# A two-layer graph network kernel: the residual sum ahead of the gated products on VectorE, and TensorE's output banks released by the gated products

## The chip, the cores and the metric

One core of one Trainium2 chip runs the whole kernel. The metric is the device time of one execution in microseconds, as the median over runs. The engines are TensorE (PE in the profile, PEld for its weight loads), VectorE (DVE), ScalarE (ACT), GpSimd (POOL) and SyncE (SP). Each runs its own stream of instructions in order, and they are tied together by semaphores: one engine's instruction raises one when it completes, another engine's stream waits for a count.

## The reference, cut to what matters

There are 50,000 nodes with 160 features (64 scalars and 32 vectors of 3) and 50,000 edges sorted by destination. Two layers follow each other, each with a layer norm and a ReLU in front.

```python
h = maximum(layernorm(x), 0)
x = x + L0(h, edge_attr_4, edge_attr_8)     # first layer, gated
h = maximum(layernorm(x), 0)
x = x + L1(h, node_vec1, edge_attr_4, edge_attr_10)

# L0, cut:
xs, xv = s @ W1_s, v @ W1_v                 # of the node rows
w = silu(edge_embed @ fc_w1 + b1) @ fc_w2 + b2
msg = [products of w, xs[src], xv[src] and edge_sh]     # 384 per edge
agg = segment_sum(msg, dst)
out_s, out_v = agg_s @ W2_s + s @ Wsc_s, agg_v @ W2_v + v @ Wsc_v
scalars, gates = silu(out_s[:, :64]), silu(out_s[:, 64:96])
return node_features + [scalars, out_v * gates]
```

The change is in the end of the first layer: `out_v * gates` is the gated product, and `x + node_features` is the residual sum that the new rows start from.

## The kernel before, in words

The code counts its layers from 0 (`first` is true in the layer that the change is about). The node range is cut into 10 lanes, and one turn handles a pair of tiles, 128 edges each, of two lanes. There are 205 turns, and after them a short second pass (`finish`, `t.serial`) for destinations with too many edges.

The turns are a software pipeline written out by hand. `run_steps` calls `step(T)` once for each step s on each engine, and `T(k)` is turn s-k, or nothing where that doesn't exist. So in one step an engine works on several turns at different stages, and the order of the lines in `step` is the order of its stream.

In the first layer a turn goes through these stages. T(0): the gathered rows `xg` and the node rows `xn` are in, VectorE takes their statistics (`stats`, `means`) and subtracts the mean (`edge_h`, L1138), GpSimd makes the inverse deviations (`rstd`). T(1): ScalarE makes the node's normed rows `hn` (`node_h`, L1404) and TensorE transposes (`transposes`). T(2): TensorE computes the radial hidden layer (`radial`, L1567) and the edge products (`edges`), ScalarE copies them to SBUF (`copy_xw`: L1422, then two scaled pieces in L1429), VectorE adds `xn` and `hn` into `kept` (`residual`, L1148). T(3): VectorE makes the messages (`products` from L1214 on, `messages`). T(4): TensorE sums them by destination (`sums`). T(5): TensorE multiplies the sums by the output weights (`outputs`, L1622) into `out_ps`, and ScalarE takes the SiLU of the gates and scalars (`gates`, L1458). T(6): VectorE multiplies the vectors by the gates (`gated_vectors`, L1241, which reads `out_ps`, the last reader of its first 192 columns), and adds the result to the residual sum (`new_rows`, L1251, which reads SBUF alone); then statistics for the second layer's norm (`stats2`, `means2`, with GpSimd's `rstd2`, L1082 and L1084). T(7): VectorE's `scales2` (L1281), ScalarE's `node_h2`, TensorE's `transposes2` (L1639). T(8): TensorE's `pre` (L1651) makes the second layer's node products in other columns of the same banks, ScalarE scales them out (`scale_pre`, L1483) and stores them (`base_tab`, issued on its own queue, L1511). T(9): SP stores the new rows to `table` (L968).

`kept` has 8 slots (`RING`). `residual` overwrites a slot, so it waits for the stores of the turn 8 before (`stored[t.slot]`), and for `hn_ready`. `outputs` has to wait until `out_ps` is free: in the first layer `deep` is 1, so it waits for the `rows_ready` of the turn before, which `new_rows` raises. `pre` waits for `rows_ready` of a turn that `outputs`, just ahead of it in the same step, has waited for already. `gated_ready` is raised by `gated_vectors`; before, only `new_rows` waits for it.

Every third step up to step 123, VectorE also advances the plan of the lanes in pieces between the other work: `lanes.reach` (needs a gather of GpSimd), `clip`, `count`, `advance`, `keep`. Each piece waits for the piece before it.

## Time and profile before

| | us |
|---|---|
| median of 3 runs | 2412.83 |
| lowest and highest | 2403.69, 2425.43 |
| the profiled execution | 2389.98 |
| its span, first to last instruction | 2388.2 |

Over the span TensorE is busy for 91%, its weight loads for 86%, ScalarE 81%, VectorE 80%, GpSimd 65%. The first layer's turns run from about 60 us to 1500 us, the second layer's from about 1560 us to the end. The granted TensorE clock is 0.968 of full speed over the span (2.4 GHz is full), and 0.99 to 1.00 from 400 us to 1500 us.

How to read the rows that follow: a timeline row has the start in us from the span's first instruction, the busy time in us, the engine, the line of the kernel, the operation, its tiles as out<-in, and the count merged into the row. A bracket at its end is time in which the engine stood idle just before, with what ended it. Where a row merges two or more instructions of an engine, the time is of all of them together. Starts on one engine can be closer than the busy times, since the next instruction starts while the last one completes.

### The profile page before, as it was taken

To read this page: it belongs to the slowest core of one execution; us is meant where nothing else is said; L and a number is where in the kernel's file an instruction comes from. 1 tells how busy PE (TensorE), PEld (TensorE's weight loads), DVE (VectorE), ACT (ScalarE), POOL (GpSimd) and SP (SyncE) were. 2 spreads that over 40 slices of the span, in tenths; PEclk is the share of its full clock that TensorE was granted. 3 is DMA by queue.
4 is the path that set the end of the run, shared out by engine and by line. 5 is a ranking of instruction groups with operands and counts; after the bars stand their busy time and mean duration, and the time that the engine had idled before them with its cause. 6 is when DMAs were issued, how large, how long until landed. Compare 5 with 4: busy or idle time off the path is not lost. (4 is left out here: it accounts for less than half of the span.)

```text
span 2388.2 us, 79221 instructions
## 1 busy us (share of the span) xinstructions
PE 2176.7 (91%) x22003; PEld 2045.3 (86%) x22004; DVE 1909.6 (80%) x8636; ACT 1930.8 (81%) x5167; POOL 1541.1 (65%) x1925
## 2 busy tenths in 40 slices
PE   0889999999999999999999999559999999999997
PEld 0788888889999899899999999359999998999996
DVE  5878998789899898898889988227777777777775
ACT  2677898788888888798889988338888888888885
POOL 4766888778878887777777776145555554554550
PEclk9999999999999999999999999669999999999998
DMA  5456557644445545444444443247777776776772
GB/s 156 90 147 146 142 146 204 175 125 131 126 129 132 125 131 134 116 132 132 132 127 132 133 131 105 64 111 191 190 189 191 190 188 178 189 186 176 197 189 76
DMA packets 498819, 351.30 MB, mean 147 GB/s; under 512 B 188108, under 2 KB 484030, under 8 KB 498382
## 3 DMA queue, kind: packets, MB, share of 16 engines
q1 hardware_dynamic: 401007, 209.61, 34.3%
q0 software_dynamic: 41472, 69.42, 13.0%
q10 hardware_dynamic: 55904, 67.22, 8.1%
q8 instruction: 182, 2.98, 0.5%
q14 instruction: 254, 2.08, 0.3%
HBM read 199.00 MB, written 151.77 MB: 147 GB/s over the span
## 5 line engine op out<-in xcount | busy, mean ns | idle before, releaser
L1060 POOL DMA_INDIRECT xg<-table,from_row x411 | 397.9, 968 | 422.3 <-DVE msg L1233 229.1
L1622 PE MATMUL out_ps<-w_out,aggT 128*128 128x128 f32 (+1 forms) x4932 | 604.6, 273 | 17.4 <-issue 14.3
L1622 PEld LDWEIGHTS out_ps<-w_out,aggT 128*128 128x128 f32 x4932 | 591.6, 194 | 21.3 <-issue 19.4
L1060 POOL DMA_INDIRECT xg<-in_x,win x411 | 484.7, 1179 | 148.8 <-issue 127.5
L1607 PE MATMUL agg_ps<-sel,msg 128*128 128x128 f32 x3708 | 525.9, 284 | 27.5 <-issue 16.0
L1607 PEld LDWEIGHTS agg_ps<-sel,msg 128*128 128x128 f32 x3708 | 463.4, 195 | 37.0 <-issue 25.2
L1438 ACT ACTIVATE msg<-pw,win 128x64 f32<-128x64 f32 x1233 | 341.3, 352 | 5.2 <-issue 2.9
L1449 ACT COPY aggT<-agg_ps 128x768 f32<-128x768 f32 (+1 forms) x310 | 247.4, 798 | 96.0 <-PE agg_ps L1607 56.6
L1073 POOL TENSOR_TENSOR rs<-ve,neghalf 128x4 f32<-128x4 f32 x206 | 224.2, 1088 | 17.1
L1404 ACT ACTIVATE hn<-xn,nmr,rs 128x192 f32<-128x192 f32 x411 | 201.2, 540 | 41.5 <-DVE nmr L1165 41.2
L1483 ACT ACTIVATE kept<-out_ps,a_sb 128x320 f32<-128x320 f32 x410 | 193.9, 525 | 49.0 <-PE out_ps L1651 35.0
L1422 ACT COPY xw_sb<-front_ps 128x512 f32<-128x512 f32 x206 | 120.6, 586 | 112.4 <-PE front_ps L1639 91.1
L1082 POOL TENSOR_SCALAR ve<-mv 128x2 f32<-128x2 f32 x206 | 76.8, 373 | 205.3 <-DVE mv L1274 170.4
L1466 ACT ACTIVATE h<-kept,nmr,rs 128x192 f32<-128x192 f32 x411 | 201.7, 546 | 3.6 <-DVE nmr L1281 3.6
L1257 DVE SCALAR_TENSOR_TENSOR kept<-out_ps,a_sb,kept 128x160 f32<-128x160 f32 x410 | 138.4, 379 | 73.3 <-PE out_ps L1622 37.5
L1241 DVE TENSOR_TENSOR fe<-out_ps,fe 128x192 f32<-128x192 f32 x206 | 73.4, 356 | 150.4 <-ACT fe L1458 143.1
L1592 PE MATMUL front_ps<-w_fc,hid 100*128 100x192 f32 x822 | 182.2, 345 | 11.0 <-issue 10.0
L1651 PE MATMUL out_ps<-w_pre,hT 64*128 64x128 f32 (+1 forms) x2466 | 185.3, 281 | 5.8 <-ACT hT L1475 5.3
L1583 PE MATMUL front_ps<-w_lin,hT 64*128 64x64 f32 (+1 forms) x2466 | 174.9, 273 | 8.0 <-issue 3.8
L1629 PE MATMUL out_ps<-w_sc,hT 64*128 64x96 f32 (+2 forms) x2466 | 179.8, 278 | 0.0
L1084 POOL TENSOR_TENSOR rs<-ve,neghalf 128x2 f32<-128x2 f32 x206 | 168.1, 816 | 17.2
L1607 PE MATMUL front_ps<-sel,msg 128*128 128x128 f32 x1224 | 161.5, 282 | 17.1 <-issue 13.2
(194 smaller groups left out, 5039.2 us busy)
## 6 DMA issues: line engine op xcount, KB each, us to landing
base_tab<-kept ACTq DMA_DIRECT2D x205, 320.0 KB
kept<-base_tab SPq DMA_DIRECT2D x205, 320.0 KB
xn<-in_x SPq DMA_DIRECT2D x411, 80.5 KB, 1.8
table<-kept SPq DMA_DIRECT2D x410, 80.0 KB
out<-kept SPq DMA_DIRECT2D x410, 80.0 KB
ee_sb<-ee_parts SPq DMA_DIRECT2D x411, 22.5 KB, 1.8
ee_parts<-part SPq DMA_DIRECT2D x45, 196.0 KB
ee_sb<-ee_parts SPq DMA_DIRECT2D x411, 18.0 KB
```

Of the source, the lines that this page charges most:

```text
L1060: pool.indirect_dma_start(out=xg[:, t.slot, j, 0:D], out_offset=None, in_=edge_rows, in_offset=bass.IndirectOffsetOnAxis(ap=at, axis=0)).t ...
L1073: pool.tensor_tensor(rs[:, t.half, :, 0:b], ve[:, :, 0:b], neghalf[:, 0:2 * b].rearrange("p (a b) -> p a b", a=2), ALU.pow).then_inc(rs_re ...
L1404: ins = act.activation(hn[0:NT, t.half, :, j, :], in_parts(xn[0:NT, t.slot, j, :]), ACT.Relu, bias=nmr[0:NT, t.half, j:j + 1], scale=rs[0: ...
L1438: ins = act.activation(msg[:, t.half, j, 1 + c, 0:MUL0], pw[:, j, :], ACT.Copy, scale=harmonics(t)[:, j, 1 + c:2 + c])
L1449: act.copy(aggT[:, t.half, 0:b, :, :], sums_ps[t.half][:, 0:b, 0:BLOCKS * NT].rearrange("p j (k n) -> p j k n", k=BLOCKS)).then_inc(aggT_c ...
L1466: ins = act.activation(h2[:, :, j, :], in_parts(kept[:, t.slot, j, 2 * D:]), ACT.Relu, bias=nmr2[:, t.half, j:j + 1], scale=rs2[:, t.half, ...
L1483: act.activation(kept[:, t.slot, j, 0:2 * D].rearrange("p (k c) -> p k c", k=2), pre_ps[0:NT, j, :, :], ACT.Copy, scale=node_attr(t, j)).t ...
L1592: ins = pe.matmul(w_ps[:, j, :], hid[0:hidden, t.half, j, :], w["fc2_"][:, :], start=True, stop=True)
L1607: ins = pe.matmul(sums_ps[t.half][:, j, k * NT:(k + 1) * NT], flat[:, t.half, j, k * P:(k + 1) * P], sel[:, t.half, j, :], start=not t.ser ...
L1622: ins = pe.matmul(rows[0:NT, j, c0:c1], aggT[:, t.half, j, k, :], w[f"out{k}_"][:, :], start=fresh, stop=True, skip_group_check=not fresh)
L1629: ins = pe.matmul(rows[0:NT, j, c0:c1], hT[r, t.slot, n0:n0 + NT], w["sc"][r, c0:c1], start=False, stop=True, skip_group_check=True)
L1651: ins = pe.matmul(pre_ps[0:NT, j, :, c0:c1], hT2[r, c * NT:(c + 1) * NT], pre_w[r, 2 * c0:2 * c1].rearrange("p (k c) -> p k c", k=2), star ...
```

## The change

In VectorE's step of the first layer, `lanes.reach` and `residual` move from behind `gated_vectors` and `scales2` to ahead of them. On TensorE, `outputs` in the first layer and `pre` wait for `gated_ready` where they waited for `rows_ready`, with the same counts. The second layer's `outputs` waits as before. No instruction is added or removed.

```diff
             def step(T):
                 s = lanes.of_turn(T(0).n) if first and T(0) else None
+                if s:
+                    lanes.reach(dve, s)
+                if (t := T(2)) and first:
+                    residual(t)
                 if (t := T(6)) and first:
                     gated_vectors(t)
                 if (t := T(7)) and first:
                     scales2(t)
-                if s:
-                    lanes.reach(dve, s)
-                if (t := T(2)) and first:
-                    residual(t)
                 if s:
                     lanes.clip(dve)
                 if t := T(6):
@@
             def outputs(t):

                 pe.wait_ge(aggT_copied, t.m + 1)
-                hold(pe, rows_ready, t.freed_m(deep))
+                hold(pe, gated_ready if first else rows_ready, t.freed_m(deep))
                 if first:
                     hold(pe, ev_ready, t.m * PAIR if t.serial else (t.n - 3) * PAIR)
@@
                 pe.wait_ge(hT2_copied, t.m + 1)
                 hold(pe, ev_ready, t.m * PAIR)
-                pe.wait_ge(rows_ready, t.m + 1 if t.serial else min(t.n + 3, NB))
+                pe.wait_ge(gated_ready, t.m + 1 if t.serial else min(t.n + 3, NB))
```

## Rows read from the trace of the kernel before

**Rows 1.** Timeline, a regular turn and the start of the next: start, us, engine, line.

```profile
1350.24 0.98 ACT L1404 ACTIVATE hn<-xn,nmr,rs 128x192 f32<-128x192 f32 x2
1351.26 0.55 DVE L1138 TENSOR_TENSOR he<-xg,mv 128x384 f32<-128x384 f32 x1
...
1352.12 0.33 ACT L1458 ACTIVATE fe<-out_ps 128x192 f32<-128x192 f32 x1
...
1352.48 0.36 DVE L1241 TENSOR_TENSOR fe<-out_ps,fe 128x192 f32<-128x192 f32 x1 [0.67 <-ACT fe L1458]
...
1352.76 0.15 DVE L1281 SCALAR_TENSOR_TENSOR nmr<-mv,rs 128x2 f32<-128x2 f32 x1
1352.83 0.55 DVE L1148 TENSOR_TENSOR kept<-xn,hn 128x384 f32<-128x384 f32 x1
1352.92 0.59 ACT L1422 COPY xw_sb<-front_ps 128x512 f32<-128x512 f32 x1 [0.47 <-PE front_ps L1639]
...
1353.30 0.48 DVE L1251 TENSOR_TENSOR kept<-kept,fe 128x320 f32<-128x320 f32 x1
...
1353.70 0.28 DVE L1214 TENSOR_TENSOR pw<-xw_sb 128x128 f32<-128x128 f32 x1
...
1354.12 0.27 PE L1567 MATMUL front_ps<-ee_sb,fc_parts 75*128 75x128 bf16 x2
...
1354.96 1.45 PE L1622 MATMUL out_ps<-w_out,aggT 128*128 128x128 f32 x12
...
1358.90 0.55 PE L1639 MATMUL front_ps<-ident,h 128*128 128x128 f32 x3
...
1359.58 0.59 ACT L1422 COPY xw_sb<-front_ps 128x512 f32<-128x512 f32 x1 [0.47 <-PE front_ps L1639]
...
1360.78 0.27 PE L1567 MATMUL front_ps<-ee_sb,fc_parts 75*128 75x128 bf16 x2
```

**Rows 2.** Windows for L1241 alone: stretch, length, busy (x turns), PEclk, DMA, GB/s.

```profile
205.00:530.00 325.00, 15.65 (x44) 0.98 0.61 158
530.00:910.00 380.00, 19.62 (x55) 1.00 0.50 129
1210.00:1370.00 160.00, 8.58 (x24) 1.00 0.49 132
```

**Rows 3.** Waits, 200 to 1500 us: engine, waiting line, releaser, total, times, longest.

```profile
DVE fe L1241 <- ACT fe L1458: 122.4, 171, 2.8
DVE kept L1148 <- DMA table<-kept: 11.6, 11, 2.9
DVE nmr L1281 <- POOL rs L1084: 3.8, 9, 0.6
...
PE out_ps L1622 <- issue: 6.5, 4, 2.7
```

**Rows 4.** Timeline around a step in which the residual waits for a store.

```profile
464.78 0.56 DVE L1148 TENSOR_TENSOR kept<-xn,hn 128x384 f32<-128x384 f32 x1 [2.93 <-DMA table<-kept]
465.32 0.47 DVE L1251 TENSOR_TENSOR kept<-kept,fe 128x320 f32<-128x320 f32 x1
465.90 1.79 PE L1622 MATMUL out_ps<-w_out,aggT 128*128 128x128 f32 x12 [2.20 <-issue]
```

**Rows 5.** Timeline around a step in which GpSimd is late.

```profile
826.08 1.50 POOL L1082 TENSOR_SCALAR ve<-mv 128x2 f32<-128x2 f32 x1 [0.29 <-issue]
...
826.94 0.55 DVE L1138 TENSOR_TENSOR he<-xg,mv 128x384 f32<-128x384 f32 x1
...
827.68 0.36 DVE L1241 TENSOR_TENSOR fe<-out_ps,fe 128x192 f32<-128x192 f32 x1 [0.20 <-ACT fe L1458]
...
828.42 0.16 DVE L1281 SCALAR_TENSOR_TENSOR nmr<-mv,rs 128x2 f32<-128x2 f32 x1 [0.38 <-POOL rs L1084]
...
832.72 0.24 POOL L1082 TENSOR_SCALAR ve<-mv 128x2 f32<-128x2 f32 x1
...
834.53 0.36 DVE L1241 TENSOR_TENSOR fe<-out_ps,fe 128x192 f32<-128x192 f32 x1 [0.32 <-ACT fe L1458]
...
841.64 0.36 DVE L1241 TENSOR_TENSOR fe<-out_ps,fe 128x192 f32<-128x192 f32 x1 [1.13 <-ACT fe L1458]
```

## The prediction

> **What bounds the kernel now.** I read the timeline of a regular turn first, because the first layer is one turn repeated 205 times and the change touches nothing in the second layer's turns. The reader should look for a closed loop, a chain of releases that comes back to its own start one turn later. There is one, between TensorE and ScalarE [rows 1]. `radial` starts at 1354.12. TensorE then works through its step without a pause to `transposes2`, which starts at 1358.90 and ends at 1359.45. ScalarE's copy starts 0.13 behind that, at 1359.58, and its three pieces release the next `radial` at 1360.78. The loop is 1360.78 - 1354.12 = 6.66 us: 5.33 of TensorE, 0.13, and 1.20 of ScalarE and its semaphore. VectorE is on no link of it.
>
> Second, where VectorE stands in that turn. It ends `edge_h` at 1351.81 and is idle for 0.67 us until ScalarE's gates let `gated_vectors` start at 1352.48 [rows 1]. Over 1300 us it waits there 171 times, 122.4 us in all [rows 3], far more than in any other place. So VectorE has about 0.67 us of room in a 6.66 us turn, and `new_rows` ends at 1353.78 while `outputs` starts at 1354.96 [rows 1]: 1.18 us of room on the wait that the change moves. A wait of a given total is worth nothing by itself, if the engine that waits isn't on the loop.
>
> Third, how many turns are regular. A count of `gated_vectors` gives 160/24 = 6.67 us for a late stretch, 380/55 = 6.91 for the middle and 325/44 = 7.39 for the early one [rows 2]. Against 6.67 that is 55 x 0.24 = 13 us and 44 x 0.72 = 32 us, so 45 us lie in irregular turns. Only there can VectorE decide anything.
>
> **The change part by part.**
>
> **Residual first, regular turn.** `residual` now follows `edge_h`. Its input `hn` is complete at 1350.24 + 0.98 = 1351.22, ahead of `edge_h`'s end, and the step from one VectorE start to the next is about 0.47 here (1352.83 to 1353.30), so it runs at about 1351.8 to 1352.3, in the idle time [rows 1]. The gates still end at 1352.45, so `gated_vectors` stays at 1352.48. Then `scales2` at 1352.76, and `new_rows` at about 1352.9 (it must wait for the end of `gated_vectors`, 1352.84) instead of 1353.30. `products` could go at 1353.3, but it needs ScalarE's copy, which ends at 1352.92 + 0.59 = 1353.51. It went at 1353.70, so it gains 0.16 us, not 0.47. The rest shows up as a new wait of VectorE for the copy, about 0.2 us a turn. Nobody on the loop waits for VectorE in a regular turn, so this is worth 0. If this cover were gone (no idle time before the gates), the order wouldn't matter at all, since VectorE would do the same work back to back.
>
> **`reach` first.** It is one small VectorE instruction in 41 steps, moved over two others. Its input comes from a GpSimd gather issued two steps before, and no wait for it stands among the waits. I take 0.
>
> **The release of `out_ps`.** `gated_vectors` ends 0.94 us before `new_rows` in the old order (1352.84 against 1353.78), but `outputs` has 1.18 us of room, so a regular turn gains 0 [rows 1]. It counts where `outputs` really follows `new_rows`. TensorE stood before `outputs` 4 times, 6.5 us in all [rows 3]. One such place is a step in which `residual` waited for a store until 464.78, and `new_rows` ended at 465.79, 0.11 before `outputs` at 465.90 [rows 4]. In the new order `gated_vectors` is behind that same wait: it starts 0.47 after 464.78 and ends at 465.61, so `outputs` comes at 465.72, a gain of 0.18 only. The bounds for one place are 0.18 and 0.94, so 0.7 to 3.8 us for four. I take three at 0.18 and one at 0.94: -1.5 us. For `pre`, `outputs` in the same step has passed the same count, before and after: 0.
>
> **Turns in which GpSimd is late.** `scales2` waited for GpSimd 9 times, 3.8 us [rows 3]. In the one shown, it started 828.42 - 827.68 = 0.74 after `gated_vectors` instead of 0.28, and everything behind it was 0.46 late [rows 5]. The next two turns took 834.53 - 827.68 = 6.85 and 841.64 - 834.53 = 7.11, 13.96 together, against 2 x 6.91 for the stretch and 2 x 6.67 for regular ones. So 0.46 us of lateness costs between 0.14 and 0.62; I take 0.4. In the new order `residual` is already done, `new_rows` follows `scales2` by 0.08 and not 0.54, and `products` comes at 827.68 + 0.74 + 0.08 + 0.40 = 828.90. That is 1.22 behind `gated_vectors`, exactly where a regular turn has it today. So most of the lateness is absorbed: between 0 and 9 x 0.62 = 5.6 us, and with 0.3 a time I take -2.7 us.
>
> **Turns in which the store is late.** `residual` waited for the store 11 times, 11.6 us [rows 3]. This wait is now ahead of `gated_vectors` and `scales2`. What is queued behind it: the gated product, for which TensorE's `outputs` waits, and `scales2`, for which ScalarE's `node_h2` waits more than 3 us later. The end of the wait is set by the store and doesn't move. Behind it `new_rows` came after 0.47 before; now `gated_vectors`, `scales2` and the semaphore stand between, 0.47 + 0.28 + 0.08 = 0.83. VectorE is 0.36 us later, and by the rate above (0.4 for 0.46) that costs 0.3: 11 x 0.3 = +3.3 us. The residual also starts about 1.0 us sooner (1352.83 against 1351.8), so stores that land in that last microsecond become waits too; only those in the last 0.3 make `products` later than now. How many these are, no view shows. From none to as many again gives 0 to 3.3 more. I take 0.7, so +4.0.
>
> **GpSimd's reads of SBUF.** `residual` moves next to `edge_h`, where GpSimd runs `rstd`. The trace has a GpSimd instruction of 0.24 us (832.72) that took 1.50 us, to 827.58, when it fell into VectorE's run of products; that run ended with `edge_h` at 827.49 [rows 5]. The moved sum makes the run 0.47 longer. In a regular turn GpSimd has room, so I take 0, and the bound is the rival below. The Trainium skill, SBUF — State Buffer, "SBUF: two separate sides", says that a VectorE instruction with two SBUF inputs and a GpSimd instruction that reads SBUF exclude each other for their whole length. The trace agrees with it in this one place. By that rule every one of GpSimd's three small instructions behind `edge_h` would wait out the residual, some 0.5 us a turn; by the row of a regular turn they need not.
>
> **The sum.** 0 - 1.5 - 2.7 + 4.0 = -0.2 us, which is nothing. The profiled execution's own 2389.98 us (span 2388.2 and 1.8 around it) would become 2389.8. The median of the runs is 22.85 us above that execution, so I forecast 2412.83 - 0.2, rounded to 2412 us.
>
> **The rivals.**
>
> **A, no change** (the sum above). For it speaks that the 6.66 loop has no VectorE link. Its own range is 2402 to 2424, which is about the spread of the runs.
>
> **B, VectorE's lateness makes the irregular turns.** If more of the 45 us than I counted come from VectorE being tight in steps with the plan's extra instructions, the room that it gains gives back about half, 24 us: 2389. For it: the middle stretch is 0.24 a turn above regular, and the plan's steps are in it. Against it: VectorE waited for the gates 171 times in 188 turns, so it had room nearly everywhere [rows 3].
>
> **C, GpSimd is shut out by the longer run (slower).** One mechanism: in the steps up to 123, in which GpSimd also gathers for the plan, L1082 falls into VectorE's run and takes 1.50 instead of 0.24, now up to 2.0. It decides once `scales2` starts more than 0.28 + 0.36 = 0.64 behind `gated_vectors`, since `products` then misses the copy. At 0.4 us each in one of three steps this is 41 x 0.4 = 16 us (2429), in two of three 33 us (2445). I take 2439 as its middle. Against it: only 9 of 188 turns show the wait today. The rule named above speaks for it, and it is this rival.
>
> **D, late stores.** The wait now holds back the gated product, and a late `outputs` makes the next store late. If all 11 cost their 0.36 in full and twice as many join them, this is 33 x 0.36 = 12 us: 2425.
>
> **How the numbers follow.** A 0.60, B 0.14, C 0.12, D 0.14. About 1% is what a measurement can tell from no change: below 2389 is faster, above 2437 slower. Faster takes most of B: 0.11. Slower takes half of C and a little of D: 0.08. The same is the rest, 0.81. The range holds A and D and the nearer halves of B and C, 2390 to 2430.
>
> **What would show it.** Right: VectorE's wait for the gates falls from 122 us to under 70 in the same window, a new wait of `products` for the copy of L1422 of some 30 us appears, regular turns stay at 6.66, `new_rows` starts 0.4 behind `gated_vectors`. B would show as fewer us a turn in the middle stretch, with regular turns unchanged. C would show as more L1082 of over 1 us and more waits of L1281 for L1084. D would show as more and longer waits of L1148 for the store, and more idle time before L1622. The forecast is wrong if a regular turn is no longer 6.66 us, in either direction, because then VectorE or GpSimd does have a link in the loop that I didn't see.

## The result: 0.8% slower

| kernel | median, us | runs | ratio to before, 95% interval |
| --- | --- | --- | --- |
| before, same chip | 2413.52 (2400.29 to 2434.57) | 20 | 1 |
| after | 2436.39 (2412.08 to 2446.94) | 20 | 1.0083 (1.0056 to 1.0109) |

The ratio is worked out from all runs, not from the two medians (their quotient is 1.0095). The forecast was 2412 us with a range of 2390 to 2430, so the measured time lies above the range.

The profiled execution of the changed kernel took 2438.15 us (span 2436.4), that of before 2389.98, which is less than any of the 20 runs in the table. So this pair of executions lies further apart (48.2 us) than the medians do (23). Of the 48.2 us, 38.2 lie in layer 1: from the first gated product to the 205th it takes 1464.7 us, against 1426.5. Another 13.7 lie in layer 2 (from its first to its last new row 801.5 us against 787.8), which the change doesn't touch. Layer 2 took 785 to 806 us in the twelve profiles of such chips, whatever the kernel.

I looked first for what had been forecast. These are the waits of after in the same window as [rows 3] (engine, waiting line, releaser: total us, times, longest).

```profile
DVE fe L1241 <- ACT fe L1458: 48.0, 126, 0.7
PE front_ps L1567 <- ACT xw_sb L1429: 42.3, 65, 1.7
DVE pw L1214 <- ACT xw_sb L1422: 22.8, 120, 1.5
DVE kept L1148 <- DMA table<-kept: 21.7, 19, 5.6
PE out_ps L1622 <- issue: 9.8, 5, 3.7
DVE nmr L1281 <- POOL rs L1084: 1.6, 3, 0.7
ACT aggT L1449 <- PE agg_ps L1607: 52.0, 62, 1.7
```

VectorE's wait for the gates fell from 122.4 to 48.0 us, and the new wait of `products` for ScalarE's copy came, 22.8 us. All that VectorE was to do, it did. The line that nobody had asked about is the last one: ScalarE's copy of the sums waits 52.0 us for TensorE, 62 times. In the trace of before the same line reads:

```profile
ACT aggT L1449 <- PE agg_ps L1607: 9.7, 14, 1.6
```

The windows for L1241 (length, busy time and turns, PEclk, DMA, GB/s) have fewer turns in every stretch: 42, 54 and 23, against 44, 55 and 24 in [rows 2].

```profile
205.00:530.00 325.00, 14.91 (x42) 0.97 0.59 153
530.00:910.00 380.00, 19.22 (x54) 1.00 0.49 125
1210.00:1370.00 160.00, 8.22 (x23) 1.00 0.48 128
```

The timeline shows what a long turn looks like. First a regular turn of after, 1354.74 - 1348.09 = 6.65 us (start, us, engine, line, operation; in brackets the idle time before it and what ended it):

```profile
1348.09 0.36 DVE L1241 TENSOR_TENSOR fe<-out_ps,fe 128x192 f32<-128x192 f32 x1 [0.35 <-ACT fe L1458]
...
1348.48 0.49 DVE L1251 TENSOR_TENSOR kept<-kept,fe 128x320 f32<-128x320 f32 x1
...
1349.13 1.09 POOL L1060 DMA_INDIRECT xg<-in_x,win  x1 [0.18 <-issue]
1349.14 0.31 DVE L1214 TENSOR_TENSOR pw<-xw_sb 128x128 f32<-128x128 f32 x1 [0.17 <-ACT xw_sb L1422]
...
1349.64 0.55 DVE L1219 TENSOR_TENSOR msg<-pw,she 128x384 f32<-128x384 f32 x1
...
1349.84 0.89 PE L1607 MATMUL agg_ps<-sel,msg 128*128 128x128 f32 x6
1350.52 0.94 POOL L1060 DMA_INDIRECT xg<-in_x,win  x1 [0.30 <-issue]
1350.76 0.80 ACT L1449 COPY aggT<-agg_ps 128x768 f32<-128x768 f32 x1
```

Then a long one, 1292.81 - 1285.09 = 7.72 us:

```profile
1285.09 0.36 DVE L1241 TENSOR_TENSOR fe<-out_ps,fe 128x192 f32<-128x192 f32 x1 [0.35 <-ACT fe L1458]
...
1286.84 0.89 PE L1607 MATMUL agg_ps<-sel,msg 128*128 128x128 f32 x6
...
1287.42 0.01 SPq L934 DMA_DIRECT2D win<-in_edge_rec  x1
...
1287.52 0.96 POOL L1060 DMA_INDIRECT xg<-in_x,win  x1 [0.31 <-issue]
1287.56 1.45 PE L1622 MATMUL out_ps<-w_out,aggT 128*128 128x128 f32 x12
...
1288.19 0.02 SPq L938 DMA_DIRECT2D ee_sb<-ee_parts  x1
...
1289.01 0.80 ACT L1449 COPY aggT<-agg_ps 128x768 f32<-128x768 f32 x1 [1.34 <-PE agg_ps L1607]
...
1291.83 0.56 DVE L1148 TENSOR_TENSOR kept<-xn,hn 128x384 f32<-128x384 f32 x1 [0.89 <-ACT hn L1404]
...
1292.81 0.36 DVE L1241 TENSOR_TENSOR fe<-out_ps,fe 128x192 f32<-128x192 f32 x1 [0.42 <-ACT fe L1458]
```

TensorE's last group of sums starts at 1349.84 in the one and at 1286.84 in the other, and in both its own next group follows at the usual pitch (1287.56 here). But the copy that only needs the completion of that group starts 0.92 us behind the group's start in the regular turn, and 2.17 behind it here. ScalarE stood idle for 1.34 us of that. From there the delay goes through ScalarE's chain: its copy L1422 starts at 1293.24, and the next `radial`, on the closed loop of [rows 1], waits 1.07 us for it:

```profile
1294.45 0.27 PE L1567 MATMUL front_ps<-ee_sb,fc_parts 75*128 75x128 bf16 x2 [1.07 <-ACT xw_sb L1429]
```

So TensorE does its work on time, and its completion reaches ScalarE late. ScalarE itself is not what stands still: the trace also records when the semaphore was raised. In the long turn this is at 1288.98, 1.53 us behind the start of the last matmul of the sums, and the copy starts 0.02 behind it. In regular turns of before and after it is 0.29 us behind that start. In all 63 late turns of after whose update is recorded it came 0.49 us or more behind it, and the copy followed by 0.02 each time.

I counted late turns in the decoded trace. A turn is **late** where the copy L1449 starts more than 0.15 us behind both of two moments: the start of the last matmul of the sums + 0.31 us (the usual distance; that matmul starts some 0.6 us behind the group) and the end of ScalarE's own previous instruction. Between 200 and 1480 us before has 15 late turns with 12.0 us of lateness, after has 72 with 58.7 us. The difference, 46.7 us, stands against 38.2 us that layer 1 grew by, so a part of the lateness costs nothing. The delays of after stand in two groups: 40 of the 72 are between 0.15 and 0.6 us, and 20 are between 1.2 and 1.3.

What did the change move at that place? Not TensorE. GpSimd's first gather runs beside VectorE's products and ends 0.02 to 0.03 us behind the end of one of them, L1219 (1349.64 + 0.55 = 1350.19 and 1350.22 in the regular turn above). That product now comes earlier, with the whole run of products (0.16 us, as a median over the regular turns), and the second gather starts 0.31 us behind the end of the first. This is a regular turn of before at the same place, with L1219 ending at 1354.72:

```profile
1353.36 1.38 POOL L1060 DMA_INDIRECT xg<-in_x,win  x1 [0.17 <-issue]
...
1354.17 0.55 DVE L1219 TENSOR_TENSOR msg<-pw,she 128x384 f32<-128x384 f32 x1
...
1354.23 0.89 PE L1607 MATMUL agg_ps<-sel,msg 128*128 128x128 f32 x6
...
1355.05 0.95 POOL L1060 DMA_INDIRECT xg<-in_x,win  x1 [0.31 <-issue]
1355.16 0.80 ACT L1449 COPY aggT<-agg_ps 128x768 f32<-128x768 f32 x1
```

The second gather starts 1355.05 - 1354.23 = 0.82 us behind the group of sums; in after it is 1350.52 - 1349.84 = 0.68. Against the last matmul of the sums that is 0.21 and 0.08 us. I call this distance the **phase** of the turn. Not every turn has its gathers at this place. In the counts the phase is that of the gather that starts nearest to the matmul, and in some turns this is the first of the two. In before 3 of the 77 turns at a phase near 0.2 are late (72 of them have the second gather there, 2 of these are late); in after 28 of the 42 near 0.1 are (second gather: 22 of 36). That gave the theory which the experiments start from: the phase of the second gather decides whether TensorE's completion comes late.

### The profile page after: what moved, and what is told of

Read it like the earlier page. It is cut to its first block and busy times, and to the rows that moved or that the text cites. A ratio compares the mean times of both kernels' runs of the same rounds, so it can differ in the third digit from the quotient of the medians.

```text
span 2436.4 us, 79221 instructions
## 1 busy us (share of the span) xinstructions
PE 2189.6 (90%) x22003; PEld 2055.2 (84%) x22004; DVE 1936.0 (79%) x8636; ACT 1923.0 (79%) x5167; POOL 1514.8 (62%) x1925
## 5 line engine op out<-in xcount | busy, mean ns | idle before, releaser
L1622 PE MATMUL out_ps<-w_out,aggT 128*128 128x128 f32 (+1 forms) x4932 | 603.7, 273 | 20.9 <-issue 14.4
L1622 PEld LDWEIGHTS out_ps<-w_out,aggT 128*128 128x128 f32 x4932 | 590.5, 194 | 25.3 <-issue 16.8
L1060 POOL DMA_INDIRECT xg<-in_x,win x411 | 433.5, 1055 | 147.7 <-issue 128.0
L1449 ACT COPY aggT<-agg_ps 128x768 f32<-128x768 f32 (+1 forms) x310 | 247.2, 797 | 136.8 <-PE agg_ps L1607 94.6
L1082 POOL TENSOR_SCALAR ve<-mv 128x2 f32<-128x2 f32 x206 | 68.7, 334 | 266.8 <-DVE mv L1274 214.8
L1483 ACT ACTIVATE kept<-out_ps,a_sb 128x320 f32<-128x320 f32 x410 | 192.7, 522 | 41.1 <-PE out_ps L1651 32.7
L1422 ACT COPY xw_sb<-front_ps 128x512 f32<-128x512 f32 x206 | 120.6, 585 | 111.5 <-PE front_ps L1639 80.4
L1651 PE MATMUL out_ps<-w_pre,hT 64*128 64x128 f32 (+1 forms) x2466 | 191.7, 284 | 6.2 <-ACT hT L1475 4.9
L1629 PE MATMUL out_ps<-w_sc,hT 64*128 64x96 f32 (+2 forms) x2466 | 180.0, 279 | 0.0
L1148 DVE TENSOR_TENSOR kept<-xn,hn 128x384 f32<-128x384 f32 x206 | 113.7, 552 | 81.9 <-DMA table<-kept 37.3
```

Of the source, the lines that this page charges most:

```text
L1060: pool.indirect_dma_start(out=xg[:, t.slot, j, 0:D], out_offset=None, in_=edge_rows, in_offset=bass.IndirectOffsetOnAxis(ap=at, axis=0)).t ...
L1449: act.copy(aggT[:, t.half, 0:b, :, :], sums_ps[t.half][:, 0:b, 0:BLOCKS * NT].rearrange("p j (k n) -> p j k n", k=BLOCKS)).then_inc(aggT_c ...
L1483: act.activation(kept[:, t.slot, j, 0:2 * D].rearrange("p (k c) -> p k c", k=2), pre_ps[0:NT, j, :, :], ACT.Copy, scale=node_attr(t, j)).t ...
L1622: ins = pe.matmul(rows[0:NT, j, c0:c1], aggT[:, t.half, j, k, :], w[f"out{k}_"][:, :], start=fresh, stop=True, skip_group_check=not fresh)
L1629: ins = pe.matmul(rows[0:NT, j, c0:c1], hT[r, t.slot, n0:n0 + NT], w["sc"][r, c0:c1], start=False, stop=True, skip_group_check=True)
L1651: ins = pe.matmul(pre_ps[0:NT, j, :, c0:c1], hT2[r, c * NT:(c + 1) * NT], pre_w[r, 2 * c0:2 * c1].rearrange("p (k c) -> p k c", k=2), star ...
```

## The experiments

The table gives all eighteen kernels, in sets that ran side by side on one chip. Each kernel has its ratio to runs of before on the same chip. "Late" is the count of late turns and their sum in us between 200 and 1480 us of the profiled execution, "layer 1" its time from the first to the 205th gated product.

| set | kernel | before there | ratio, 95% interval | late | layer 1 |
| --- | --- | --- | --- | --- | --- |
| - | (before, first profile) | 2413.52 | 1 | 15, 12.0 | 1426.5 |
| - | (after, first profile) | 2413.52 | 1.0083 (1.0056 to 1.0109) | 72, 58.7 | 1464.7 |
| 1 | release_only | 2402.95 | 0.9959 (0.9934 to 0.9985) | 16, 13.7 | 1429.1 |
| 1 | order_only | 2402.95 | 1.0140 (1.0096 to 1.0185) | 83, 56.5 | 1456.1 |
| 1 | gap_gathers | 2402.95 | 0.9977 (0.9946 to 1.0008) | 22, 25.2 | 1431.7 |
| 1 | late_products | 2402.95 | 1.0054 (1.0026 to 1.0082) | 71, 49.7 | 1454.4 |
| 2 | sp_later | 2302.45 | 0.9977 (0.9961 to 0.9993) | 0 | 1411.7 |
| 2 | rel_sp_later | 2302.45 | 1.0001 (0.9989 to 1.0013) | 0 | 1413.2 |
| 2 | sp_nudge | 2302.45 | 1.0026 (1.0007 to 1.0045) | 0 | 1419.5 |
| 2 | small_gap | 2302.45 | 0.9961 (0.9945 to 0.9978) | 0 | 1419.1 |
| 3 | after_again | 2405.64 | 1.0100 (1.0047 to 1.0153) | 78, 67.0 | 1465.3 |
| 3 | sp_later_b | 2405.64 | 1.0111 (1.0068 to 1.0155) | 85, 71.7 | 1466.7 |
| 3 | sp_nudge_b | 2405.64 | 1.0025 (0.9984 to 1.0066) | 33, 28.8 | 1454.0 |
| 4 | small_gap_b | 2413.12 | 1.0056 (1.0029 to 1.0083) | 81, 65.1 | 1462.6 |
| 4 | after_attr | 2413.12 | 1.0041 (1.0015 to 1.0068) | 51, 59.8 | 1454.8 |
| 4 | rel_attr | 2413.12 | 0.9998 (0.9970 to 1.0026) | 29, 42.4 | 1446.1 |
| 5 | after_c | 2304.17 | 0.9986 (0.9966 to 1.0006) | 0 | 1410.0 |
| 5 | release_only_b | 2304.17 | 0.9980 (0.9962 to 0.9998) | 0 | 1418.5 |
| 5 | wide_gap | 2304.17 | 1.0010 (0.9993 to 1.0027) | 0 | 1414.8 |
| 5 | rel_wide_gap | 2304.17 | 1.0056 (1.0032 to 1.0080) | 0 | 1429.5 |

**Which half of the change loses?** Two kernels with one half each. release_only:

```diff
-                hold(pe, rows_ready, t.freed_m(deep))
+                hold(pe, gated_ready if first else rows_ready, t.freed_m(deep))
...
-                pe.wait_ge(rows_ready, t.m + 1 if t.serial else min(t.n + 3, NB))
+                pe.wait_ge(gated_ready, t.m + 1 if t.serial else min(t.n + 3, NB))
```

> The kernel before with only the second half of the change: TensorE's outputs and pre matmuls wait for the gated products instead of the new rows; VectorE's order is that of before. Phase theory (the loss comes from when GpSimd's second gather instruction starts against the last matmul of the sums, and VectorE's order sets that): VectorE and GpSimd keep the phases of before, the second gather starts 0.2 us behind the start of the last sums matmul in most turns, about 15 turns of layer 1 have a late signal between 200 and 1480 us, and the ratio is 0.997 to 1.002. Rival, the release is the cause (TensorE starts its outputs at other moments and its signals come late): 60 or more late turns and a ratio of about 1.008.

order_only is the kernel after with exactly these two lines put back.

> The kernel after with TensorE's two waits put back to the new rows, so that only VectorE's order is changed. Phase theory: products start about 0.16 us earlier as in the changed kernel, GpSimd's second gather starts about 0.1 us behind the start of the last sums matmul, 60 to 80 late signals between 200 and 1480 us, ratio 1.006 to 1.012. Rival, the release is the cause: about 15 late turns, ratio 0.998 to 1.003.

Measured: 0.9959 and 1.0140, with 16 and 83 late turns. The release is a gain, VectorE's order is the loss, and 0.9959 x 1.0140 = 1.0099 is what both together give within their intervals. The rival that the release is the cause has fallen. Both ratios lie outside what was expected, below 0.997 and above 1.012, because the gain of the release was not thought of.

**Is it VectorE, or GpSimd behind it?** gap_gathers leaves VectorE and TensorE as they are in after and moves the second gather alone:

```diff
                 for j in range(t.tiles):
                     at = win[:, t.place, j, 0:1] if first else from_row[:, t.place, j:j + 1]
+                    if first and not t.serial and j == 1:
+                        pool.memset(v["pad"][:, t.half, :], 0.0)     # pad: [P, 2, 256]
```

> The changed kernel with a memset of 128x256 on GpSimd (estimated 0.3 us) between the two gather instructions of each turn of layer 1; VectorE and TensorE are as in the changed kernel. Phase theory: the second gather starts 0.35 to 0.45 us behind the start of the last sums matmul, where the changed kernel has 2 late signals in 31 turns; late turns fall from 72 to under 25, and the time to that of the kernel before or a little under it, ratio 0.990 to 1.001. Rival, VectorE's new order itself delays TensorE's signals or something that follows them: still 60 or more late turns, ratio 1.008 or, with 205 extra instructions on GpSimd, more.

Measured: 0.9977 and 22 late turns. The timeline of this kernel:

```profile
1346.72 0.89 PE L1610 MATMUL agg_ps<-sel,msg 128*128 128x128 f32 x6
1347.12 0.33 POOL L1062 MEMSET pad<- 128x256 f32 x1
1347.62 0.96 POOL L1063 DMA_INDIRECT xg<-in_x,win  x1 [0.16 <-issue]
1347.64 0.80 ACT L1452 COPY aggT<-agg_ps 128x768 f32<-128x768 f32 x1
```

The second gather now starts 0.90 us behind the group in place of 0.68, which is a phase of 0.29, and the copy comes at its 0.92. Of the 61 turns at this phase none is late. VectorE's own row tells that it has the order of after: it waits for the gates as in after, 46.7 us against 48.0. With 205 instructions more on GpSimd the loss is gone, so VectorE's order costs little directly; most of its cost goes through what GpSimd does when. Where the first gather is the nearest one, moving the second changes nothing: in this kernel 10 of the 11 such turns with phases of 0.02 to 0.12 are still late.

```profile
DVE fe L1244 <- ACT fe L1461: 46.7, 121, 2.4
ACT aggT L1452 <- PE agg_ps L1610: 17.7, 21, 1.6
```

**Does bringing VectorE's run back help?** late_products adds one instruction to VectorE in after:

```diff
                 if t := T(3):
+                    if first:
+                        dve.tensor_tensor(v["pad"][:, t.half, :], zeros[:, 0:260], zeros[:, 0:260], ALU.add)
                     products(t)
```

> The changed kernel with one more VectorE instruction directly ahead of the products of each turn of layer 1 (an addition of 128x260 zeros to a scratch tile, estimated 0.33 us), of which 0.17 us lie in the wait for ScalarE's copy and 0.16 us put the products back to where the kernel before has them. Phase theory: VectorE's run of products and GpSimd's gathers come back to the phases of before (second gather 0.2 us behind the start of the last sums matmul), about 15 to 25 late turns, ratio 0.998 to 1.003. Rival, VectorE's order or the early release is the cause whatever the phase: 60 or more late turns and a ratio of 1.008 or more, up to 1.02 if VectorE's extra 0.33 us a turn were on the path.

Measured: 1.0054 and 71 late turns, a miss for the theory in its simple form. The products went back by 0.09 us only (they start 1.21 ahead of the last matmul of the sums; 1.30 in after, 1.15 in before), and 33 of the 56 turns with phases near 0.2 and 0.3 are late, where before has 3 of 77 near 0.2. With the second gather alone it is no different: 22 of the 39 turns that have it 0.14 to 0.21 us behind the matmul are late. So the phase of the second gather is not all. What else decides stayed open.

**Are SyncE's issues needed?** In the long turn above SyncE's issues come at 1287.42, 1288.19 and 1288.94, in bursts 0.76 us apart, where an issue usually takes 0.33. Issues of under 0.1 us stand near the sums (from 1 us ahead of their last matmul to 2 us behind it) in 54 of the 72 late turns of after, and in 56 of the other 106. So the collision might be between SyncE and GpSimd. sp_later puts SyncE's loads behind the place (rel_sp_later is release_only with the same lines):

```diff
                 hold(sp, hid_done, t.freed(RING))
+                if first and not t.serial:
+                    hold(sp, aggT_copied, t.n - AHEAD - 4)
```

> The changed kernel in which SyncE's loads of layer 1 also wait for ScalarE's copy of the sums of the turn that runs, so that they are issued from about 1.1 us behind the start of the last sums matmul instead of from 0.9 us before to 0.9 us behind it. The loads are needed three turns later. VectorE, GpSimd and TensorE are as in the changed kernel: the second gather still starts 0.1 us behind that matmul. Theory that the late signal needs SyncE's issues and GpSimd's gathers together: late signals of the sums fall from 72 to under 15 and the ratio to 0.990 to 0.999. Rival, the gather's phase alone delays the signal: 60 or more late turns and a ratio of 1.006 to 1.010. Rival, loads that come later cost something themselves: few late turns, and still a ratio above 1.003.

> The kernel before with the second half of the change (TensorE's two waits on the gated products) and with SyncE's loads of layer 1 behind the copy of the sums as in sp_later; VectorE's order is that of before. This is the candidate for a version that beats both kernels. Theory (SyncE's issues and GpSimd's gathers together make the late signals): the 16 late turns of release_only fall to under 8 and the ratio is 0.985 to 0.995. Rival (what is late in release_only comes of the gathers alone): as release_only, 0.996.

sp_nudge is the kernel before with two increments that nobody waits for:

```diff
                     load_waits(t)
+                    if first:
+                        for _ in range(2):
+                            sp.sem_inc(passed, 1)
```

> The kernel before with two semaphore increments that nobody waits for on SyncE ahead of the loads of each turn of layer 1, so that the loads are issued some 0.1 us later; the rest is that of before. In before the load that is issued 0.51 us ahead of the last sums matmul ends 0.07 us before the first gather ends and takes 0.35 us in all of 36 regular turns; in the changed kernel, whose first gather ends 0.12 us earlier, it is stretched. Theory of the collision: now this load is still being issued when the gather ends, is stretched in most turns as in the changed kernel, and some of the signals behind come late: 40 or more late turns, ratio 1.003 to 1.010. Rival, only what VectorE or GpSimd do matters: 15 late turns, ratio 0.998 to 1.002.

And small_gap is gap_gathers with a `pad` of 16 in place of 256 columns:

> As gap_gathers, with a memset of 128x16 (estimated 0.1 us) in place of 128x256 between the two gathers: the second one starts about 0.2 us behind the start of the last sums matmul, where the kernel before has it, with the first gather still ending 0.12 us earlier than in before. If the start of the second gather against TensorE's signal is what decides: about 15 to 25 late turns, ratio 0.993 to 1.000, as gap_gathers. If the time between SyncE's stretched load (it ends 0.03 us ahead of the matmul) and the second gather decides, as in late_products, where 33 of 56 turns at 0.2 to 0.3 us were late: 40 or more late turns, ratio 1.002 to 1.008.

This set ran on another chip, and told something else than it was made for: before runs there in 2302.45 us, 4% faster, and not one turn is late in any of the four kernels, though the second gather of sp_later and small_gap has its phase of 0.10 in 52 turns each. The late completions depend on the chip. Nothing of the questions above was answered, so sp_later and sp_nudge were run again, with the changed kernel as a control.

> The changed kernel itself, as a control. The kernel before ran at 2403 to 2414 us on the chips of the first two comparisons and at 2302 us on the chip of the third, and on that one no signal of TensorE's sums came late in any kernel. If this chip is of the first kind (before near 2400 us): 60 to 80 late signals between 200 and 1480 us, ratio 1.005 to 1.012. If it is of the second kind (before near 2300 us): no late signal, ratio 0.996 to 1.001; the rival there, that VectorE's order costs something of its own without late signals, gives 1.005 or more.

> The changed kernel with SyncE's loads behind the copy of the sums, as sp_later, here beside the changed kernel on the same chip. On a chip with late signals (before near 2400 us): theory that they need SyncE's issues and GpSimd's gathers together, under 15 late turns and 0.985 to 0.999; rival, the gather's phase alone, 60 or more late turns and 1.006 to 1.010. On a chip without them (before near 2300 us): 0.998, as the changed kernel.

> The kernel before with SyncE's loads some 0.1 us later, as sp_nudge. On a chip with late signals (before near 2400 us): theory of the collision, the load issued 0.4 us ahead of the last sums matmul is stretched over the end of the first gather, 40 or more late turns, 1.003 to 1.010; rival, only what VectorE or GpSimd do matters, 15 late turns and 0.998 to 1.002. On a chip without them: no late signal and 1.001 to 1.004, as before.

Here before took 2405.64, and late turns were back: 78 in the control, ratio 1.0100. sp_later_b has 85 and 1.0111. Its loads were moved behind the place, and 30 of 32 turns with a phase near 0.1 were late. In 44 of its 85 late turns SyncE issues nothing at all within 0.9 us of the last matmul of the sums. So SyncE's issues are not needed: that theory is gone, and what the bursts in SyncE's row come from stays open. sp_nudge_b, 1.0025 (0.9984 to 1.0066) with 33 late turns, is under the 40 that were expected, and the same edit gave 1.0026 on the chip without late turns. It settles nothing.

**How far must the second gather move, and does useful work do it?** small_gap_b is small_gap again; after_attr moves GpSimd's copy of the node attributes out of `rstd` and between the gathers, and rel_attr does so in release_only:

```diff
                 for j in range(t.tiles):
+                    if first and not t.serial and j == 1:
+                        wait_apart(pool, xn_in[t.slot], (t.uses + 1) * 16 * t.tiles, passed)
+                        pool.tensor_copy(a_sb[:, t.n, :], xn[:, t.slot, :, D]).then_inc(attr_kept, 1)
...
-                if not t.serial:
-                    pool.tensor_copy(a_sb[:, t.n, :], xn[:, t.slot, :, D]).then_inc(attr_kept, 1)
```

> The changed kernel with a memset of 128x16 between the two gathers of a turn. On a chip with late signals (before near 2400 us): if the start of the second gather alone decides, its 0.2 us is where the kernel before has 1 to 3 late turns in 77, so 20 to 30 late turns in all and a ratio of 0.995 to 1.001. If the end of the first gather or what VectorE's order does to it counts as well, as in late_products (33 of 56 late at 0.2 to 0.3 us): 50 or more late turns, 1.003 to 1.010. On a chip without late signals (before near 2300 us): none, 0.995 to 0.998 as measured there.

> The changed kernel in which GpSimd's copy of the node attributes (0.40 us a turn) stands between the two gathers of a turn in place of behind the second; no instruction is added but its wait for the node rows. The second gather starts about 0.45 us behind the last sums matmul, where 0 of 135 turns were late. On a chip with late signals: the phase theory expects 20 to 30 late turns and a ratio of 0.990 to 0.999; the rival, that the extra room on GpSimd's queue in gap_gathers worked in another way, expects 1.003 or more. On a chip without late signals: none, 0.994 to 0.999.

> The kernel before with TensorE's two waits on the gated products (0.996 of before by release_only) and with the copy of the node attributes between the two gathers; VectorE's order is that of before. The candidate for a kernel that beats both. The second gather starts about 0.6 us behind the last sums matmul. On a chip with late signals: 16 late turns become under 8, ratio 0.987 to 0.996; rival, GpSimd's pair of gathers ending 0.4 us later costs something of its own (the second gather's rows land later), 0.998 or more. On a chip without late signals: 0.995 to 1.001.

small_gap_b: the memset of 128x16 takes 0.13 us but fits into the 0.31 us that pass between the two gathers anyway, so the phase stayed at 0.09, and so did the 81 late turns and the loss, 1.0056. It is no dose between the others, but a control: with an instruction more on GpSimd that doesn't move the gather, as many turns are late as in after (after itself did not run on this chip). after_attr is a miss. With the copy out of `rstd`, GpSimd came earlier to its first gather (1.59 us ahead of the last matmul, not 1.31), and the usual phase of the second became -0.07 and not 0.45. There 10 of 56 turns are late, but all 22 at phases of -0.27 and -0.22 are, with delays up to 2.4 us. In 21 of these 22 the gather at the matmul is the first of the two. rel_attr shows the same: 18 of 20 late near -0.25 (19 of them with the first gather there), and only 1 of 77 at 0.08, the very phase at which after is late in most turns; there it is nearly always the second gather. So after_attr has fewer late turns than after, 51, but the same sum of lateness, 59.8 us, and rel_attr has more than release_only in both, 29 and 42.4 us. The late turns moved to another phase, and mostly to the other gather, instead of going away. Both kernels came out above the ratios that the theory gave them, and rel_attr (0.9998) is where its rival had it.

**A square on one chip.** The last set was to hold order and gap against each other, with the release in all four.

> The changed kernel once more, as the control of this chip. On a chip with late signals (before near 2400 us): 70 to 80 late turns, 1.006 to 1.011. On one without (before near 2300 us): none, and 0.995 to 1.000, since the kernels built on it gave 0.996 and 0.998 there; the rival that VectorE's order costs something by itself gives 1.003 or more.

> As release_only: the order of before with TensorE's two waits on the gated products. On a chip with late signals 15 to 20 late turns and 0.994 to 0.999 again; without them 0.998 to 1.002.

wide_gap is gap_gathers with a `pad` of 440 columns, rel_wide_gap the same in release_only.

> The changed kernel with a memset of 128x440 between the two gathers. The one of 128x256 takes 0.33 us and moved the second gather by 0.21 us, the one of 128x16 takes 0.13 us and moved it by nothing, so this one (estimated 0.50 us) moves it by 0.38 us: from 0.08 to 0.46 us behind the last sums matmul, and the group of turns at -0.20 to 0.18. Theory (the loss is the late signals and the second gather's moment sets them): under 25 late turns, 0.990 to 0.999 on a chip with late signals. Rival (the moment matters only with others, as in after_attr): 40 or more, 1.002 to 1.008. Without late signals: 0.994 to 0.999.

> The kernel release_only with the same memset of 128x440 between the gathers: the second gather moves from 0.21 to 0.59 us, the groups at -0.19 and -0.11 us to 0.2 and 0.3. On a chip with late signals: late turns from 16 to under 10 and a ratio of 0.990 to 0.996 of before; the rival is that the later rows of the second gather cost what the signals give back, 0.996 to 1.000. Without late signals: 0.997 to 1.002.

Before took 2304.17 here, and again no turn was late. The waits of after_c, 200 to 1500 us:

```profile
DVE fe L1241 <- ACT fe L1458: 41.1, 105, 2.8
DVE kept L1148 <- DMA table<-kept: 31.7, 25, 3.8
DVE pw L1214 <- ACT xw_sb L1422: 23.8, 116, 1.5
DVE nmr L1281 <- POOL rs L1084: 11.9, 12, 1.8
PE front_ps L1567 <- ACT xw_sb L1429: 8.0, 16, 1.2
ACT aggT L1449 <- PE agg_ps L1607: 4.9, 10, 1.2
```

VectorE does there what it does in after (41.1 and 23.8 us, against 48.0 and 22.8), the second gather has its phase of 0.10 in 54 turns, and the copy of the sums waits 4.9 us in all. The ratio is 0.9986 (0.9966 to 1.0006). The rival that VectorE's order costs something by itself has fallen: after_c and release_only_b differ by 1.3 us of 2300. The gaps cost time here, 0.2% and 0.8% above the kernels that they are made from, and both came out above what was expected without late signals (1.0010 against at most 0.999, 1.0056 against at most 1.002). Whether the wide gap pays where turns are late was not found out, since this chip has none.

**What the runs show, and what they don't.** Shown: the loss is VectorE's order and not the release; it exists only where TensorE's completion of the sums comes late, on the chips where before takes 2403 to 2414 us; a change on GpSimd alone takes most of the late turns and the loss away; neither the release nor SyncE's loads are needed for it. In the twelve rows of the table with late turns, layer 1 broadly grows with their sum, from 1426.5 us at 12.0 to 1466.7 at 71.7; a straight line through them gives 0.65 us of layer 1 for 1 us of lateness. Not shown: by what path a gather holds up the completion, and that the second gather is the one that does it. This pools the nine profiles with late turns of the first comparison and of sets 1 and 3, with both orders, 477 late turns in 1613, and keeps the turns apart by which of the two gathers is the nearest:

| phase (nearest gather), us | late turns, second gather nearest | late turns, first gather nearest |
| --- | --- | --- |
| -0.30 to -0.14 | 63 of 127 | 22 of 33 |
| -0.14 to 0.02 | 30 of 77 | 28 of 51 |
| 0.02 to 0.10 | 88 of 132 | 48 of 49 |
| 0.14 to 0.22, VectorE's order of before | 2 of 193 | 4 of 44 |
| 0.14 to 0.22, VectorE's order of after (no gap, no added instruction) | 4 of 4 | 18 of 21 |
| 0.42 and more | 3 of 190 | 0 of 91 |

So a start of either gather near the last matmul goes with late completions. The change moved the second gather of its regular turns from a row with 2 of 193 into the one with 88 of 132. Of the turns in the ranges left out of the table, 0.10 to 0.14 and 0.22 to 0.42, 19 of 56 and 37 of 205 are late. But the phase is not all. The two rows at 0.14 to 0.22 and rel_attr's 1 of 77 at 0.08 say that a second condition counts, and 84 late turns have their nearest gather more than 0.3 us ahead of the matmul. Where the first gather ends may be the second condition in the turns with the second gather at the matmul (0.10 us ahead of the last matmul in before, 0.22 in after, 0.50 in rel_attr), but late_products doesn't order itself by that, and it can't be it where the first gather is the one at the matmul. This stays open.

## Why the prediction was wrong

**The loop and VectorE's place beside it: right.** A regular turn is 6.65 us in after, `new_rows` starts 0.39 us behind `gated_vectors` (1348.48 - 1348.09), the wait for the gates fell to 48.0 us (forecast: under 70), and the new wait for the copy is 22.8 us (forecast: some 30). On the chips without late completions the whole sum held as well: it gave -0.2 us, and after_c measured 0.9986, that is -3 us with an interval from -8 to +1.

**The step that failed** is "Nobody on the loop waits for VectorE in a regular turn, so this is worth 0", together with "In a regular turn GpSimd has room, so I take 0". Both sentences price only lateness: whether somebody waits longer for VectorE, or GpSimd misses its hour. Here the products came 0.16 us earlier, GpSimd's second gather 0.14 us earlier, nobody missed anything, and with the earlier gather a third engine's signal came late, which is on the loop: 72 turns with 58.7 us of lateness in place of 15 with 12.0, and a ratio of 1.0140 for the order by itself (order_only). I had the 0.16 us in the text and did not follow them to who starts when VectorE's run ends. Why the gather's start goes with the late signal stays open. Of the 204 turns of layer 1 only 82 are under 6.7 us in after, against 124 in before. I had also written that the forecast would be wrong if a regular turn was no longer 6.66 us. It is still 6.65; what changed is how many turns are regular, and that test could not see it.

**The release of `out_ps`: right in sign, too small.** Taken as -1.5 us out of bounds of 0.7 to 3.8; release_only measured -0.41% (0.15 to 0.66%), some 10 us, and release_only_b -0.20% (0.02 to 0.38%), some 5 us. The wait that was priced is smaller there: TensorE's wait in front of `outputs` fell from 6.5 us, 4 times [rows 3], to 1.8 us, once, in release_only. That would account for 4.7 us. But layer 1, where the change acts, is not shorter in the profile of release_only (1429.1 us against 1426.5, on another chip), so where the 10 us lie isn't shown.

**Turns in which GpSimd is late: not more of them, price not shown.** `scales2` waited for GpSimd 9 times in before [rows 3] and 3 times in after. With no late signals it is 20 times, 22.1 us, in release_only_b and 12 times, 11.9 us, in after_c. The forecast was that the same waits would cost less; no run prices that.

**GpSimd's small instructions: the zero hid a shift.** From the row of a regular turn I took that they need not wait out the residual. One of them does: L1071 takes 0.54 us in the median turn of after against 0.23 in before, and in the turn above it starts at 1347.29 and ends at 1347.83, 0.09 behind the residual's end. So the first gather of a regular turn starts later against the sums (1.32 us ahead of their last matmul in place of 1.48), while it ends earlier. GpSimd had the room, as I said, but its gathers moved, one later and one earlier.

**Late stores: as forecast in kind.** The residual's wait for a store went from 11 times, 11.6 us [rows 3], to 19 times, 21.7 us. On the chip of after_c it was 25 times, 31.7 us, against 22 times, 28.5 us in release_only_b, and the kernels took the same time. So nothing says that the term of +4.0 us was too small.

**The rivals.** B did not come. Both signs of D did, on a small scale: more waits for the store, and TensorE's idle time before L1622 went from 6.5 us, 4 times, to 9.8 us, 5 times. That is far from the loss, and the square on the last chip has the longer waits without a loss. C named the right engine and the right time (2429 to 2445, with its middle at 2437 and not at the 2439 that I took; it is 2436.39) for a wrong reason. It said that GpSimd's short instruction L1082 would be shut out longer and `scales2` would come late; L1082 took over 1 us 9 times in before (one of them in [rows 5]) and 3 times in after, and `scales2` waited less. A rival that hits the number by another mechanism was not right. The first gather takes 1.38 us in the regular turn of before and 1.09 in that of after, and ends 0.02 to 0.03 us behind L1219 in both. This agrees with the rule of the Trainium skill, SBUF — State Buffer, "SBUF: two separate sides", by which a VectorE instruction with two SBUF inputs and a GpSimd instruction that reads SBUF exclude each other. By that rule I asked only whether GpSimd would be held longer, and not whether it would be let go earlier.

**Which kernel to take.** release_only beats before on both kinds of chips, 0.9959 and 0.9980 with intervals just under 1. Against after it wins where signals come late (after has 1.0083 and 1.0100 there); on the other kind the two can't be told apart (0.9980 and 0.9986).

## What to carry to other kernels

An engine off the critical loop that gets faster changes when the engines behind it start, and that is a change even if nobody was waiting for it: follow the earlier time through to every instruction that it releases, and ask what stands beside that on the loop. Where a loop gets longer though every instruction on it has its old duration, look at the distance from the end of one engine's work to the start of the next one's, turn by turn. And measure a change of under 1% on more than one chip, with the kernel before beside it each time: here the same edit is about 1% slower in two comparisons and not slower in a third.

## What the hardware showed that I had not expected

- TensorE's completion of a group reaches ScalarE 0.31 us behind the start of its last matmul, or else up to 2.5 us later than that (most often 0.15 to 0.6 or 1.2 to 1.3), while TensorE itself goes on at its usual pitch. In after this happened in 72 of 178 turns; in 42 of them one of the two gathers, in 31 the second, started between 0.15 us ahead of that matmul and 0.15 us behind it.
- Not only the sums are signalled late. The last matmul of L1629 raised its semaphore over 0.2 us later than at its quickest in 54 of 176 recorded turns of before and 36 of 178 of after, that of L1651 in 23 of 184 and 10 of 179; in after_c and release_only_b both counts are 0. The lateness counted in this document is that of the sums alone.
- On the same chips SyncE at times issues in bursts 0.76 us apart (1287.42, 1288.19, 1288.94), with single issues of 0.01 us, where 0.33 is usual. Between 200 and 1480 us 141 of 1588 issues of before take under 0.1 us and 224 of 1567 of after; on the chips without late completions it is 0 of 1589 (sp_later) and 0 of 1585 (after_c).
- Chips differ by more than the change does: before took 2403 to 2414 us in four comparisons and 2302 to 2304 in two. In the profiles most of that is layer 2 (from its first to its last new row 785 to 806 us against 731) and the stretch between the layers (86 to 89 us against 68 to 72). Layer 1 of before has 1426.5 us; on the other kind of chip the kernels with its order have 1413.2 to 1419.5 without a gap.
- A memset of 128x16 between two gathers costs 0.13 us and moves nothing, since 0.31 us pass between two gathers anyway; one of 128x256 (0.33 us) moves the second by 0.21.
